# Moving the loads of the experts' input rows from SyncE's DMA queue to ScalarE's

## The reference

```
scores = softmax(x @ gate.T)               # 64 experts; 3 of 8 groups, then 6 experts per token
buf[e, pos] = x[token]                     # 96 slots per expert; what overflows shares slot 95
g, u = buf @ Wg[e].T, buf @ Wu[e].T        # [96,256] @ [256,176], for each of 64 experts
out[e] = (silu(g) * u) @ Wd[e].T           # [96,176] @ [176,256]
y[token] = sum over its 6 slots of out * weight
y + shared expert (one dense silu layer of width 352)
```

## Time and profile before

| | |
|---|---|
| three executions | 1323.67, 1330.4 and 1333.24 us, median 1330.4 |
| the profiled execution | 1323.04 us; its span 1321.3 us |
| busy share of the span | TensorE 76%, its weight loads 46%, ScalarE 55%, VectorE 40%, GpSimd 32% |
| expert stage 0 | first input load issued at 685 us, last product at 860 us |
| expert stage 1 | first input load issued at 1101 us, last product at 1281 us |

### The profile page before, as it was taken

How to read it: one execution, slowest core, us unless ns; L and a number is a source line. 1 busy time by engine, 2 the same in 40 slices (tenths; PEclk the granted TensorE clock), 3 DMA queues, 4 the chain that set the end, 5 groups by cost and what they waited for, 6 DMA issues and landing times.

```text
span 1321.3 us, 18696 instructions
## 1 busy us (share of the span) xinstructions
PE 1000.1 (76%) x6520; PEld 606.2 (46%) x6520; DVE 524.2 (40%) x1532; ACT 728.7 (55%) x960; POOL 425.4 (32%) x408
## 2 busy tenths in 40 slices
PE   5877768787887788885629988944788574988974
PEld 3533323322332333232329977822354344977862
DVE  7744531255212412311603322357675731322227
ACT  2286989999999999995104433414443301433330
POOL 3100000000230022251155545500398883544450
PEclk9877888998999998999769999957787886999895
DMA  9990000000110001000958999457032524999848
GB/s 354 395 385 3 1 0 1 0 17 6 51 51 32 1 35 59 29 13 22 272 150 230 285 257 237 65 163 250 35 113 101 174 80 120 282 256 244 200 50 313
DMA packets 94925, 176.10 MB, mean 133 GB/s; under 512 B 13118, under 2 KB 46879, under 8 KB 94832
## 3 DMA queue, kind: packets, MB, share of 16 engines
q1 hardware_dynamic: 71216, 146.48, 35.3%
q0 software_dynamic: 23616, 28.44, 10.3%
HBM read 107.30 MB, written 83.72 MB: 145 GB/s over the span
## 4 chain that ended last, share of the span: by engine, by line
PE 21%; DMA 11%; POOL 5%; SPq 5%; issue 4%; DVE 4%; ACT 2%; DVEq 1%; POOLq 0%; ACTq 0%
DMA XE<-expert_in 9%; PE PS L1339 8%; PE PS L1350 5%; POOL expert_in L307 4%; PE PS L1409 3%; SPq L1116 2%; SPq L1117 2%; PE PS L1277 2%; PE PS L1326 2%; DMA spare_space<-expert_out 1%; PE PS L1262 1%; POOL pause L315 1%; DMA normed<-xp 1%; POOL expert_out L1225 1%; DMA expert_out<-ob,yidx 0%
## 5 line engine op out<-in xcount | busy, mean ns | idle before, releaser
L307 POOL DMA_INDIRECT expert_in<-xp,didx x192 | 194.7, 1014 | 626.5 <-ACT PR L684 483.9
L679 ACT ACTIVATE PR<-PS 128x1024 f32<-128x1024 f32 (+3 forms) x320 | 275.5, 935 | 55.7 <-PE PS L578 39.7
L684 ACT ACTIVATE PR<-PR 128x2048 f32<-128x2048 f32 (+3 forms) x160 | 272.5, 1705 | 0.0
L1225 POOL DMA_INDIRECT expert_out<-ob,yidx x128 | 180.6, 1411 | 181.8 <-ACT ob L1518 132.4
L587 PE MATMUL PS<-PR,V 128*32 128x512 f32 (+3 forms) x1280 | 164.9, 590 | 80.4 <-ACT PR L684 80.3
L575 PE MATMUL PS<-QT,KT 96*128 96x512 bf16 (+3 forms) x640 | 177.5, 372 | 19.8 <-ACT PR L679 16.7
L1740 DVE SCALAR_TENSOR_TENSOR gta<-gth,PS 88x192 f32<-88x192 f32 x128 | 44.8, 350 | 220.9 <-ACT gth L1508 182.2
L575 PEld LDWEIGHTS PS<-QT,KT 96*128 96x128 bf16 x640 | 59.3, 103 | 130.3 <-ACT PR L679 89.1
L1508 ACT ACTIVATE gth<-PS 88x192 f32<-88x192 f32 x128 | 41.7, 326 | 110.7 <-PE PS L1339 107.5
L1339 PEld LDWEIGHTS PS<-XT,spare_space 128*88 128x88 f32 x960 | 95.1, 168 | 9.4 <-issue 3.1
L1339 PE MATMUL PS<-XT,spare_space 128*88 128x96 f32 x960 | 96.0, 257 | 2.1 <-ACT XT L1499 1.1
(11 more groups left out here) (257 smaller groups left out, 1390.7 us busy)
## 6 DMA issues: line engine op xcount, KB each, us to landing
spare_space<-in_wgu SPq DMA_DIRECT2D x60, 352.0 KB
expert_out<-zero SPq DMA_DIRECT2D x2, 8256.0 KB, 50.2
expert_in<-zero SPq DMA_DIRECT2D x2, 7776.0 KB, 39.1
XE<-expert_in SPq DMA_DIRECT2D x32, 486.0 KB
WGU<-in_wgu SPq DMA_DIRECT2D x44, 352.0 KB
spare_space<-expert_out SPq DMA_DIRECT2D x24, 512.0 KB, 5.9
spare_space<-in_wd SPq DMA_DIRECT2D x60, 176.0 KB
shared_space<-in_wgu SPq DMA_DIRECT2D x24, 352.0 KB
```

The source lines that it names most:

```text
L307: pool.indirect_dma_start(out=buf_d[f], out_offset=bass.IndirectOffsetOnAxis(ap=didx[b][:, r, j:j + 1], axis=0), in_=xp[b][:, r, :], in_of ...
L679: act.activation(PR[:, n % 3, 2 * pr:2 * pr + 2, cols(c, s):CW], PS[:, S0 + 2 * pr:S0 + 2 * pr + 2, cols(c, s):CW], ACT.Tanh, scale=1.0 / ...
L684: act.activation(PR[:, n % 3, :, lo:CW], PR[:, n % 3, :, lo:CW], ACT.Exp, scale=SOFT_CAP).then_inc(exp_done, 1)
L1225: pool.indirect_dma_start(out=y_d[f], out_offset=bass.IndirectOffsetOnAxis(ap=yidx[:, n % 4, j:j + 1], axis=0), in_=ob[:, i % EU, :], in_o ...
```

## The change

SyncE's `experts(f)` keeps the weights alone. The waits for `dispatched` and `last_stored` and all 16 loads of XE groups go to ScalarE's stream, and so to ScalarE's DMA queue. Groups 0 and 1 are issued ahead of turned(0), group 2 after gate(0), and group e // 4 + 3 after gate(e) for e = 3, 7, 11 and so on, each ahead of out(e-1). The waits ahead of each load are the same semaphores and values as before.

```
 # SyncE
-            def inputs(f, h): ...
             def experts(f):
-                for b in range(NXP):
-                    sp.wait_ge(dispatched[b], 16 * CT * TOPK * chunks_in(b, NC * (f + 1)))
-                sp.wait_ge(last_stored, 16 * (f + 1))
-                for h in range(3):
-                    inputs(f, h)
                 for e in range(E - RING):
-                    if e % EH == 1:
-                        inputs(f, e // EH + 3)
                     weights(f, e + RING)
-                for h in range((E - RING - 2) // EH + 4, NH):
-                    inputs(f, h)
 # ScalarE, in experts(f)
+                def inputs(h):
+                    n = f * NH + h
+                    if n >= 2:
+                        act.wait_ge(xt_psum, n - 1)
+                        act.wait_ge(meta_ready, n - 1)
+                    act.dma_start(XE[:, h % 2, :, :], buf_e[f][:, EH * h:EH * (h + 1), :]).then_inc(x_ld[h % 2], 16)
+
+                for b in range(NXP):
+                    act.wait_ge(dispatched[b], 16 * CT * TOPK * chunks_in(b, NC * (f + 1)))
+                act.wait_ge(last_stored, 16 * (f + 1))
+                inputs(0)
+                inputs(1)
                 turned(0)
                 for e in range(E):
                     gate(e)
                     if e % EH == 1 and e // EH + 1 < NH:
                         turned(e // EH + 1)
+                    if e == 0:
+                        inputs(2)
+                    if e % EH == 3 and e // EH + 3 < NH:
+                        inputs(e // EH + 3)
                     if e:
                         out(e - 1)
```

More of the change, by code:

```diff
@@ L1130, in first_spare2 @@
                     weights(f, e)
[L1132 to L1137, removed]
             def last_slots(f):
```

## The result

The changed kernel takes **1285.7 us** (median of four executions, 1283.7 to 1288.1), against 1327.0 us (median of four, 1318.2 to 1333.2) for the kernel before; the ratio is **0.975**, 95% interval 0.971 to 0.979. The profiled execution of the changed kernel took 1283.7 us, span 1281.9.

A forecast was written before the change was run, and what follows sets the result against it. The prediction took the order in SyncE's one queue, input loads behind weights, as the bound: -14.7 (stage 0) - 19.4 (stage 1) + 2 (weights) = -32 us, from 1330.4 to 1298 us, range 1288 to 1330.

The forecast's parts named there:

- The bound: TensorE's transposes in both expert stages: late XE loads cost 14.7 us in stage 0 and 19.4 us in stage 1.
- The time of the load: XE loads in ScalarE's queue: 5 to 9.4 us to land, judged from GpSimd's sends.
- landing in under 10 us: Sign expected in the changed kernel's profile for XE loads issued by ScalarE.
- the lead of 13 us: From a load's issue to its group's transposes, six experts: 14.1 us less about 1; a 9.4 us load fits.
- The weights: SyncE's weight loads, next to be late: 6.6 us to spare in stage 0, 0.6 in stage 1; 2 us charged.
- The order in one queue, not the bytes: SyncE's queue: inputs without cushion stand behind weights with some ten experts' cushion; this order was called the bound.
- ScalarE's issues: 32 DMA issues on ScalarE: 0.33 to 1.1 us each, hidden, nothing in the sum.
- The cover: ScalarE's idle times of 0.60, 0.79 and 0.86 us around a load: an issue up to some 2.1 us is hidden.
- ScalarE is held: Rival: the full queue stops ScalarE's issues up to 6.07 us each, +30 us, 1360 us; chance 0.14.
- the queues don't help: Rival: the second queue's loads are served only as the first drains, or weights run short; 1326 to 1334 us; chance 0.13.
- partial gain: Rival: the rate falls some 10% or sends throttle the experts, with waits before gate_up or on GpSimd; 1303 to 1315; chance 0.13.
- The sum: Whole kernel: -14.7 - 19.4 + 2 = -32 us, from a median of 1330.4 to 1298.

The follow-up runs named there:

- Runs 3 and 4: Kernel before with XE loads moved to ScalarE in stage 0 only, or in stage 1 only: 1302.6 us (0.984) and 1306.1 us (0.989).
- run 6: Changed kernel with each input load issued two experts later, a lead of four experts in place of six: 1318.5 us, ratio 1.000 to the kernel before.
- Runs 9 and 10: Kernel before, all loads on SyncE, from group 8 on four experts' weights earlier; the second with at most four experts' weights in flight: 1306.7 and 1306.1 us.
- run 12: Kernel before, all loads on SyncE, input loads from group 3 on cut to 16 runs of 12 bytes (result not valid): 1287.6 us, ratio 0.974.
- run 8: Changed kernel with four unused copies on ScalarE behind each input load from group 3 on: 1330.6 us, ratio 1.007 to the kernel before.
- run 7: Changed kernel with two unused copies on ScalarE behind each input load from group 3 on: 1284.6 us, ratio 0.974 to the kernel before.
- run 11: Changed kernel with the 32 input loads issued by GpSimd in its queue behind the sends: 1284.9 us, ratio 0.977 to the kernel before.

## Why the prediction came out as it did

**The bound was right, in place and size.** By the prediction the two stages lost 14.7 and 19.4 us to late loads; they gave back 14.7 and 19.3. Expert 63's gate and up was put at 841.3 for stage 0 and came at 841.29. Runs 3 and 4 show each stage's part by itself, run 6 shows that the gain goes when the loads are late again, by whatever queue.

**The time of the load.** Taken at 5 to 9.4 us from GpSimd's sends, it was 9.8 in the median and 11.0 at most, so above the range, and the sign "landing in under 10 us" held for the median but not for the slowest. The step that carried the forecast was the lead of 13 us. That the sends, which are smaller and accumulate, came so near was luck in part: by run 6 a lead of 8.4 us brought nothing, and an issue placed where 9.4 us just fit would have been late.

**The weights.** 2 us were charged, with 6.6 us to spare in stage 0 and 0.6 in stage 1. They were not needed: no wait for a DMA stands before line 1323, and the weights were in some 20 and over 11 us early. The step that was mis-sized is the rate, taken at 248 to 253 GB/s from stretches with waits, "the DMA engines are full". It was 273 and 278 in the same stretches, and 288 to 295 from 50 to 90 us after the first transposes. Runs 9 and 10 show that the second queue makes part of this, as with the loads in line the rate is 261 to 272 there, at nearly the same pace of TensorE. Why loads of 1296-byte rows beside the weights cost less than among them is not shown. Measured are 2.6 us or more in line (run 12; 2.1 in the fastest stage), and in the changed kernel 10.8 us for four experts' weights in the full stretch of stage 0, from expert 44's issue at 751.09 to expert 58's at 788.93, with a load every 9.41 us beside them. (With a rate 10% lower still, the prediction's sums give 3 and 11 us where it says 4 and 10.)

**"The order in one queue, not the bytes"** was half of the truth. With the order mended in one queue a third of the gain came. Only this one other order was tried, so whether a better one would bring more is open. The loads' room in the queue is part of the cause, and a load that waits for its buffer also stops what stands behind it.

**ScalarE's issues.** 0.31 us measured, 0.33 to 1.1 taken, nothing on the path: right. The cover was put at "some 2.1 us", though its three idle times make 2.25; it is 2.9 us by run 8, and run 7's 2.15 us stay under it. The condition of the rival "ScalarE is held" never came up: the longest of ScalarE's issues took 0.50 us while SyncE's own went up to 4.57. Twelve of ScalarE's issues began while SyncE was in one of 0.8 to 3.5 us, and took 0.31 to 0.35 us themselves (timelines of SyncE and ScalarE):

```profile
1154.08 3.47 SPq L1117 DMA_DIRECT2D spare_space<-in_wd  x1
```

```profile
1154.40 0.31 ACTq L1510 DMA_DIRECT2D XE<-expert_in  x1
```

A generator that one engine locks and the other waits for, as the Trainium skill has it ("Perfetto Trace Analysis", section "DMA Instruction — HWDGE (DVE, Sync)"), does not show as a delay in these rows.

**The queues.** The loads landed in 9.8 us and the rate rose at the same pace of TensorE, so the rival "the queues don't help", 1330 us, is out; no wait moved to line 1323, so a partial gain is out too. The Trainium skill's rule that several issuing engines save only issue time ("DMA: Bandwidth & Descriptors", section "Issuing engines are not separate DMA queues"; the prediction calls this its second rival, and it stands first in its list) would have given the 1330 and is contradicted by these landings and by run 11. The round-robin between the queues that the Trainium skill states ("DMA: Bandwidth & Descriptors", section "Queues, rings and completion order") agrees with them.

**The sum.** -32 us was forecast, a ratio of 0.976 to its base of 1330.4; measured is 0.975. The stages gave -34.0, that is the full -34.1 without the 2 us for the weights. Against the 1318 to 1323 us that the kernel before took in its many later executions the time fell by 33 to 37 us. The median of 1285.7 is 12 us below the 1298 that I named and 2.3 below the lower end of the range. Of these 12, 7 come from the base, for which I took the median of three executions (1330.4) and not the profiled 1323.0. The rest is the charge of 2 us and the middle, 6 us shorter in one profile than in the other by chance, less 2 us by which the profiled execution lies under its median. The kernel's own spread (18 us between executions) should have been in the range's lower end.

## What to carry to other kernels

When an engine waits for a small transfer that stands behind large ones with a cushion, give it a queue of its own; which engine issues it mattered little here (ScalarE or GpSimd), as long as the issue comes early enough. Count the lead in experts (or tiles) against a landing time measured under load, 9 to 11 us for 486 KB here: six experts' lead gained 2.5%, four gained nothing. Before touching the length of a queue, ask whether the late transfer is late in the queue or at the issuing engine.

## What the runs showed of the hardware

- A full queue of SyncE did not hold ScalarE's: 32 issues of 0.311 us in the median and 0.497 at most, beside issues of SyncE of up to 4.57 us. The issue runs beside ScalarE's computation (issue from 777.64 to 777.95, activation from 777.58 to 777.91), so it costs its engine less than its length.
- A DMA share of 1.0 in the busy times does not mean that the engines can do no more: it reads 1.03 at 248 GB/s and 1.06 at 295. In run 12 it is 1.02 at 282 GB/s, with a queue that never fills.

```profile
750.00:760.00 10.00, 10.00 (x93) 8.96 (x92) 3.38 (x11) 4.28 (x11) 6.21 (x5) 1.00 1.02 282
```

- The recurrence between the stages has two lengths, 241 to 243 and 247 us, with the same instructions and the same 112 to 114 us at half clock; they differ in how much of TensorE's work those fall on, 57 to 59 or 63 to 64 us.
- A stop of TensorE costs more than its idle time: in stage 1 of the kernel before 11.7 us of idle time brought 13.7 us at half clock, 6.9 us of work.
